# An attention and feed-forward block on one core: down weights fetched from ScalarE's queue, row subtractions kept out of three steps, rows taken in order

## The reference

```
x = x + layernorm(attn(layernorm(x)))        # 16 heads of 32, scores masked to one triangle
x = x + layernorm(ffn(layernorm(x)))         # silu(g) * u, 2048 wide, int32 weights with zero point 128

kqv = x @ Wqkv + bqkv;  scores = k q^T / sqrt(32), triangular mask;  out = softmax(scores) v;  out @ Wo + bo
g = x Wg^T;  u = x Wu^T;  h = silu(g) * u;  out = h Wd^T      # W = (int - 128) * scale of its row
```

## Time and profile before

| | |
|---|---|
| median of 3 runs | 1640.79 us (1640.74 to 1642.38) |
| the profiled execution: its time | 1639.89 us |
| its span | 1638.1 us |
| TensorE busy in the span | 94% |
| VectorE, ScalarE, GpSimd busy | 57%, 49%, 36% |
| the chain that ended last, by engine | TensorE 72%, VectorE 10%, GpSimd 6%, ScalarE 4%, SP's queue 3% |
| attention of the 16 groups | 87.6 to about 950 us |

### The profile page before, as it was taken

One profiled execution on the slowest core, in us unless ns is written; L12 is line 12 of the kernel. 1 busy time (PEld: TensorE's weight loads), 2 busy tenths in 40 slices (PEclk: granted clock), 3 DMA queues, 4 the chain that ended last, 5 costly groups with the idle time before them and its releaser, 6 DMA issues.

```text
span 1638.1 us, 24488 instructions
## 1 busy us (share of the span) xinstructions
PE 1544.6 (94%) x9322; PEld 641.2 (39%) x9324; DVE 939.4 (57%) x1864; ACT 795.9 (49%) x1284; POOL 592.7 (36%) x809
## 2 busy tenths in 40 slices
PE   4899999998999999999977999999999999999997
PEld 2333334333333333333322244444444444444443
DVE  5666755788756887667756333564434343434344
ACT  5356676667666776667755633232222222222222
POOL 4335664677556766755755310020000000000001
PEclk8999999999999999999988999999999999999999
DMA  4212322224411233223345431221111111111000
GB/s 181 92 50 52 77 55 53 67 64 117 105 48 35 81 106 88 61 52 95 106 137 164 108 97 45 59 97 38 47 26 52 26 52 26 52 26 52 1 26 26
DMA packets 113398, 112.26 MB, mean 69 GB/s; under 512 B 69632, under 2 KB 69632, under 8 KB 113024
## 3 DMA queue, kind: packets, MB, share of 16 engines
q1 hardware_dynamic: 113280, 110.69, 23.7%
HBM read 45.37 MB, written 25.17 MB: 43 GB/s over the span
## 4 chain that ended last, share of the span: by engine, by line
PE 72%; DVE 10%; POOL 6%; ACT 4%; issue 4%; SPq 3%; DMA 1%; POOLq 0%; ACTq 0%; DVEq 0%
PE ps L976 25%; PE ps L897 16%; PE ps L993 12%; PE ps L960 10%; PE ps L934 5%; DVE mcol L1255 4%; SPq L753 3%; POOL pt L1467 2%; PE ps L910 2%; ACT pt L1109 1%; POOL rs L1387 1%; PE ps L918 1%; DVE st L1150 1%; DVE xh L650 1%; POOL pt L1458 1%
## 5 line engine op out<-in xcount | busy, mean ns | idle before, releaser
L1109 ACT ACTIVATE pt<-ps,nrm 128x512 f32<-128x512 f32 (+1 forms) x640 | 361.5, 647 | 222.0 <-PE ps L934 208.8
L976 PE MATMUL ps<-x2in,gu 128*128 128x512 f16 x2048 | 462.4, 379 | 0.1
L1255 DVE TENSOR_REDUCE mcol<-ps 128x1 f32<-128x512 f32 (+2 forms) x636 | 318.0, 566 | 139.3 <-PE ps L918 93.1
L976 PEld LDWEIGHTS ps<-x2in,gu 128*128 128x128 f16 x2048 | 200.2, 98 | 242.0 <-ACT sg L1130 0.6
L1384 POOL TENSOR_SCALAR rs<-mv 128x1 f32<-128x1 f32 x120 | 27.2, 226 | 652.4 <-DVE mv L1154 646.1
L1326 DVE SCALAR_TENSOR_TENSOR hf<-ps,usc,sg 128x512 f32<-128x512 f32 x128 | 96.1, 751 | 259.1 <-PE ps L976 245.6
L1135 ACT ACTIVATE hh<-hf 128x512 f16<-128x512 f32 x128 | 80.7, 631 | 258.8 <-DVE hf L1326 245.2
L1467 POOL TENSOR_TENSOR pt<-pt 128x1024 f32<-128x1024 f32 x84 | 201.5, 2421 | 1.8 <-ACT pt L1109 1.8
L934 PE MATMUL ps<-qpack,kpack 98*128 98x512 f16 (+3 forms) x768 | 163.6, 331 | 29.0 <-DVE mcol L1255 25.7
L993 PE MATMUL ps<-wd,hh 128*128 128x512 f16 x496 | 188.0, 379 | 0.0
L993 PE MATMUL ps<-wd,hl 128*128 128x512 f16 x496 | 188.0, 379 | 0.0
(11 more groups left out here) (125 smaller groups left out, 1592.8 us busy)
## 6 DMA issues: line engine op xcount, KB each, us to landing
qpack<-stage SPq DMA_DIRECT2D x192, 64.0 KB, 2.0
kpack<-stage SPq DMA_DIRECT2D x192, 64.0 KB, 2.0
xr<-in_x SPq DMA_DIRECT2D x32, 256.0 KB, 2.9
x1d<-xr SPq DMA_DIRECT2D x32, 256.0 KB, 2.3
x2d<-xh SPq DMA_DIRECT2D x32, 256.0 KB, 2.3
x1in<-x1d SPq DMA_DIRECT2D x8, 1024.0 KB, 5.8
out_x<-yy SPq DMA_DIRECT2D x32, 256.0 KB, 2.0
xin<-in_x SPq DMA_DIRECT2D x24, 256.0 KB, 2.9
```

Of the source, the lines that this page charges most:

```text
L976: mm = pe.matmul(bk, GU[:, c, m, i * 128:(i + 1) * 128], x2in[:, 1 - k, p, c, :], start=p == 0 and c == 0, stop=p == 1 and c == 3)
L1109: act.activation(Pt[:, PBUF[step], h, off:512], ps[:, BANK[job], off:512], ACT.Exp, scale=esc).then_inc(s_ex, 1)
L1255: mm = dve.tensor_reduce(mcol[:, n % 2, col:col + 1], scores, AX.X, ALU.max)
```

## The change

Three things, all in the attention of the four batches.

1. The fetches of down-weight blocks 1 to 7 leave SP and go to ScalarE: `act_fetch i` stands at the start of the step behind the one in which block i-1 was converted, and first waits for that conversion.
2. In groups with g = 1 no turn is placed in steps 5, 6 and 7 (those in which GpSimd adds). And turns are taken only in the order in which their rows were normed; `untaken` is now a list.
3. In groups with g = 2 the projections are laid out otherwise: `qk` in steps 3, 5, 7, 9 instead of 1, 3, 7, 9, and the first `vproj` in step 1 instead of 0.

```diff
-        for i, s in enumerate(((0, 2, 3, 7) if b else (1, 3, 7, 9), (0, 1, 2, 3), (1, 3, 7, 9), (1, 2, 3, 8))[g]):
+        for i, s in enumerate(((0, 2, 3, 7) if b else (1, 3, 7, 9), (0, 1, 2, 3), (3, 5, 7, 9), (1, 2, 3, 8))[g]):
...
-        for i, s in enumerate(((), (7, 9), (0, 2, 4, 6, 8), (0,))[g]):
+        for i, s in enumerate(((), (7, 9), (1, 2, 4, 6, 8), (0,))[g]):
...
-    untaken = 0
+    untaken = []
...
-            if kind == "residual" and adding(step):
+            if adding(step) and (kind == "residual" or step // NS % 4 == 1 and kind in ("ln1_turn", "turn2")):
                 continue
...
-            if kind in ("ln1_norm", "norm2") and untaken == 2 or kind in cost and not free(kind, step) and (
-                    room.get(step, 99) < cost[kind]):
+            if kind in ("ln1_norm", "norm2") and len(untaken) == 2 or (
+                    kind in ("ln1_turn", "turn2") and untaken[0] != t):
                 continue
-            untaken += {"ln1_norm": 1, "norm2": 1, "ln1_turn": -1, "turn2": -1}.get(kind, 0)
+            if kind in cost and not free(kind, step) and room.get(step, 99) < cost[kind]:
+                continue
+            if kind in ("ln1_norm", "norm2"):
+                untaken.append(t)
+            if kind in ("ln1_turn", "turn2"):
+                untaken.pop(0)
...
             add(("step", n, s))
+            plan += [("act_fetch", i) for i in range(1, 8) if ffn_step(i - 1) + 1 == NS * n + s]
...
-                     for each in [("ffn_load", i)] + [("ffn_fetch", k) for k in range(24) if RAW_BEFORE[k] == i]]
+                     for each in [("ffn_load", i)] + [("ffn_fetch", k) for k in range(8, 24) if RAW_BEFORE[k] == i]]
...
+                elif kind == "act_fetch":
+                    i = a[0]
+                    e.wait_ge(s_cv["act"], i)
+                    ra, src, _ = raw_of_ffn(i)
+                    act.dma_start(ra, src).then_inc(d_raw[RAW[i]], 16)
```

## The result

The kernel after the change takes 1662.09 us in the median of its runs (1661.02 to 1662.61), beside 1640.76 for the kernel before on the same chip (1636.63 to 1642.38). The ratio is 1.0133, with a 95% interval of 1.0114 to 1.0152: slower by 21.3 us. The profiled execution took 1661.02 us with a span of 1659.3; before it was 1639.89 and 1638.1. The forecast was 1661.8 us.

A forecast was written before the change was run, and what follows sets the result against it. TensorE, with 72% of the chain that ended last, was taken as the bound. +29.2 - 0.5 - 5.7 - 2.0 = +21.0 on the profiled 1639.89 gave 1660.9, and 0.9 more for the median 1661.8 us; range 1651 to 1671.

The forecast's parts named there:

- What bounds: Whole kernel: TensorE carries 72% of the chain that ended last, so time is lost or won where TensorE waits.
- Part 1: Groups 6 and 10: ScalarE's copy for a turn waits some 14.5 us behind packs; +14.6 us each, +29.2 together.
- Part 2: Groups 2, 6 and 10: what the new layout wins and costs outside the stall, together -0.5 us.
- part 3: Groups 1, 5 and 9: no turns beside GpSimd's additions; -2.4 us each in 5 and 9, -0.9 in 1, sum -5.7.
- third case: turn2 5, now in (5,8), could meet GpSimd's last addition, some 2 us a subtraction; as a rival 1668 us, 10%.
- Part 4: Groups 12 and 13: packs(14) starts earlier, -3.7 us at (13,2); exposed fetches on ScalarE cost 0.6 each; sum -2.0.
- the turns don't stall: Rival for groups 6 and 10: ScalarE's copy isn't held, the 29.2 us goes; 1631 us, faster, 7%.
- the stall is partly refilled: Rival: VectorE, GpSimd and SP run ahead during the stall, no clock loss; 11.0 us each instead of 14.6; 1653 us, 12%.
- Contention at the new places: Rival: moved subtractions of groups 1, 5, 9 cost 2 us more each, half exposed, plus step 0's inversion; 1668 us, 10%.
- the fetches only cost: Rival: SP is held by something else at packs(14) and all seven issues are exposed, +3.7 + 2.5; 1668 us, 8%.

The follow-up runs named there:

- the fastest kernel: The kernel before with the change's row work and fetches, and packs 6, 7, 10, 11 and 14 moved late in the preceding group: 1618.95 us, ratio 0.986.
- the two missed attempts to cure it: Packs 6, 7, 10, 11, 14 moved to the end of step 4 of the preceding group: 1648.54 us on the changed kernel, 1644.15 on the kernel before.

## Why the prediction was right

**What bounds.** Right. No share of the page moved by more than 3 points, the stretch with the feed-forward layer took 690.9 us in both, and the loss lies in the two steps that the forecast named for it. Smaller differences in (6,7), (10,7), (1,8) and (9,2), and 0.7 in the start-up, it had not named.

**Part 1, the stall.** The mechanism was shown from three sides: the rules of the row work alone bring it, a third buffer moves it to another engine, and half of the issues halve it. Its size was right within a microsecond. ScalarE stood 14.96 and 14.78 us, 14.5 was forecast. Counted from the start of the exponentials of (5,9), packs(7) began after 4.33 us (forecast 4.66), and the exponentials of (6,1) after 24.74 (forecast 25.06). So the whole chain was right, with 0.3 us too much at its head. What was to be given back and what the clock was to cost lie in (6,1) and (10,1): the forecast put -1.6 and +2.6 there, so +1.0, and measured are +0.5 and +0.8. Which of the two terms was off can't be told apart. In the second window above TensorE was busy for 5.12 of 6.2 us at a clock of 0.58, so it was not the bound in all of it, which points to the clock as the term that was too high. In sum a stall was worth 13.8 us in group 6 and 13.9 in group 10, for 14.6.

**Part 2, the layout.** Right in size by luck, incomplete in its reasoning. The forecast for step 0 of group 2 was -0.75, and (2,0) grew by 1.04. The gain of a step 0 without its projection is real: with the new layout (10,0) takes 5.34 us in two kernels (three buffers; packs late in the group on the changed kernel), 0.63 less than the 5.97 of before. What the forecast lacked is the clock. TensorE waits the same 1.3 us in (2,0) of the changed kernel and in (10,0) of the second of these two, but only in the first does the granted clock then fall, at 205.3 us. The windows are (2,0) of the changed kernel, and (10,0) of the other with its waits:

```profile
202.23:209.25 7.02, 5.70 (x30) 1.61 (x29) 6.25 (x13) 3.15 (x6) 2.61 (x4) 0.76 0.40 98
```

```profile
642.17:647.51 5.34, 4.02 (x30) 1.42 (x29) 5.24 (x10) 4.36 (x7) 3.28 (x5) 1.00 0.67 153
```

```profile
PE ps L921 <- ACT pt L1120: 0.8, 1, 0.8
PE ps L971 <- POOL pt L1474: 0.5, 1, 0.5
```

Such a stretch at half clock lies in (2,0) in all seven kernels with the new layout, and in none of the six without it; in the kernel before TensorE is busy through the whole of it. Why (10,0) is sometimes spared is open. (2,2) gave 0.7 back and (2,5) took 0.95. Group 2 came to +1.0 for +0.5.

In groups 6 and 10, what lies outside the stall came to +0.5 and -0.4, where -0.75 and -0.25 were forecast. (10,3) lost 1.7 us, as forecast, but (6,3) only 0.8 of its 8.20, since a copy ahead of the next exponentials found its buffer's DMA not landed. And (6,7) took 1.4 us more (5.97 to 7.39), (10,7) as much, which the forecast had not: the `qk` of that step waits for tile 23, whose turn now stands in (6,6) and not in (6,4). The first row is ScalarE's at (6,3), the second TensorE's at (6,7):

```profile
456.50 0.63 ACT L1029 ACTIVATE xh<-xn 128x512 f16<-128x512 f32 x1 [1.22 <-DMA xT<-xh]
```

```profile
473.48 1.89 PE L903 MATMUL ps<-xT,wh 128*128 128x512 f16 x8 [1.27 <-DMA xT<-xh]
```

With the rules of the row work alone (6,3) is 5.65 and (6,7) 5.97, so both come only where the two parts are together. What makes tile 23 late is again the pair of part 3. Step (6,6) is one in which GpSimd adds, and the new rule keeps turns out of such steps only in groups with g = 1. The first two rows are the changed kernel's, addition and subtraction of tile 23; the third is the subtraction of the same tile in the fastest kernel, whose turn stands in the same step:

```profile
467.39 7.43 POOL L1478 TENSOR_TENSOR pt<-pt 128x1024 f32<-128x1024 f32 x3
```

```profile
467.46 2.83 DVE L656 TENSOR_TENSOR xh<-xn,xh 128x512 f16<-128x512 f32 x1
```

```profile
451.47 0.86 DVE L661 TENSOR_TENSOR xh<-xn,xh 128x512 f16<-128x512 f32 x1 [0.33 <-ACT xh L1034]
```

In the changed kernel the subtraction comes later in the step and lasts 2.0 us longer, and TensorE waits 1.27 of them. In all six kernels with both parts it takes 2.81 to 2.83 us, and in all three with the new rules and before's layout 0.85 to 0.87. That the copies of the `qk` in (6,5), new there, push ScalarE's copy back to beside the additions is my reading of the lists, not tested. The new layout paid in no kernel here: alone it cost 0.85 to 1.3 us a group.

**Part 3, no turns beside the additions.** The mechanism was right as far as it went and the size was close: (5,7) went from 9.88 to 7.17 and (9,7) from 9.88 to 7.16, 2.7 us each for 2.4 taken. GpSimd is the next limit, as forecast: TensorE now waits 1.14 us for it there. The neighbour that the term was taken from, (4,7) in the earlier trace rows, was the right one, but it held more than the forecast named. The kernel before has a stretch at half clock in (5,7), from 406.0 to 409.4 us, and another in (9,7), and neither (4,7) nor the changed kernel has one. The 12 projection matmuls of (5,7) took 4.45 us in it and take 2.76 now; the first eight of them before:

```profile
405.56 3.17 PE L897 MATMUL ps<-wh,xT 128*128 128x512 f16 x8
```

So up to 1.7 of the 2.7 us are clock that came back; it did so where the wait of 1.67 us ahead of the stretch had gone, but no run parts the two. In group 1 the forecast left this out: it gained 2.9 and not 0.9, and 2.0 of these lie in (1,8), in which the kernel before has such a stretch and the one after has none. Group 9 gained 1.0 in all, though (9,7) alone gave 2.7, since a stretch at half clock appeared in (9,2), which went from 7.12 to 8.42. These windows are, first, of before in group 1 and then, of after, in group 9:

```profile
192.00:200.00 8.00, 6.76 (x52) 2.71 (x52) 4.10 (x13) 4.90 (x10) 2.23 (x7) 0.79 0.50 116
```

```profile
613.00:620.00 7.00, 5.50 (x44) 2.67 (x45) 5.83 (x9) 5.06 (x9) 3.93 (x7) 0.76 0.61 151
```

A longer (9,2) with such a stretch stands in five more kernels with the same row work there and is missing in three others ((9,2) is 7.05 in the one with half of packs behind, 7.17 in the one with three buffers, 7.28 with the whole of packs behind). What decides it is open. The errors in groups 1 and 9 nearly cancel.

The Trainium skill's rule (SBUF — State Buffer, Who interferes with whom, the shared port pair) was carried into the forecast as a third case: turn2 5, in its new place, could meet the last addition. It does. The first row is GpSimd's, the second VectorE's, the third VectorE's next subtraction with nothing beside it:

```profile
406.18 2.38 POOL L1478 TENSOR_TENSOR pt<-pt 128x1024 f32<-128x1024 f32 x1
```

```profile
406.96 2.15 DVE L656 TENSOR_TENSOR xh<-xn,xh 128x512 f16<-128x512 f32 x1
...
413.44 0.68 DVE L656 TENSOR_TENSOR xh<-xn,xh 128x512 f16<-128x512 f32 x1
```

It took 1.5 us longer, and 1.6 us is what was left of the addition when it began (406.18 + 2.38 less 406.96), so the trace agrees with a wait for the end of one addition. The step (5,8) still lasted 5.59 us as before: VectorE had the slack. The contention is real, and here its price was nothing; in (6,6) and (10,6), which the third case did not name, it was not.

**Part 4, the fetches.** -1.5 us for -2.0. SP no longer waits for the conversions of down weights ahead of packs(14), as was forecast; one wait of 15.5 us for the last conversion is left, ahead of a fetch of a later block at 883.38. (13,2) came to 16.20 and not to 14.5, and with the fetches alone to 14.05. In the changed kernel packs(14) runs from 826.72; the first exponentials of group 13 come at 831.8, so it begins 5.1 us ahead of them where it had been 1.4 (807.42, and 808.8). But the load of tile 21, at 843.78, comes only 3.0 us earlier, for packs(14) itself took 17.1 us against 16.4:

```profile
826.72 6.18 SPq L759 DMA_DIRECT2D qpack<-stage  x8
...
843.78 0.53 SPq L722 DMA_DIRECT2D xr<-in_x  x1
```

Why the step then shrank by 2.0 and not by 3.0 is open. In kernels that leave everything up to (13,2) there as it was, the step took 16.64 and 17.54 us beside 18.21, so a microsecond of it is spread between executions. On ScalarE an exposed fetch cost 0.63 us, (12,3) going from 6.08 to 6.71, for 0.6 taken.

The other rule of the Trainium skill (DMA: Bandwidth & Descriptors, Issuing engines are not separate DMA queues) is that an issue from another engine saves only issue time, usually small. The runs decide as follows. (13,2) fell by 4.2 us with the fetches alone, seven times an issue, so the saving there is a queue that no longer waits. In (13,2) other profiles differ by 1.6 us without any such edit, so the 4.2 is uncertain by about that. Over both groups the rule's verdict of a small gain holds all the same: none that can be told from zero on the kernel before, 1.5 us in the changed kernel, some 2 in the fastest one.

**The rivals.** That the turns don't stall fell with the first timeline. That the stall is partly refilled fell too: groups 7 and 11 have their old lengths to 0.01 us, so nothing that ran ahead was kept. Contention at the new places was there: it cost nothing in (5,8), and the forecast missed the two places, (6,6) and (10,6), where TensorE waited 1.3 us in the next step for the tile; that the fetches only cost is refuted by (13,2). The errors of the terms are -2.0 in group 1, +0.5 in group 2, -0.5 in group 5, +1.4 in group 9, -1.5 for the two stalls, +1.1 for the rest of groups 6 and 10, +0.5 in groups 12 and 13, and +0.7 in the start-up. They add up to +0.2: 21.2 in the spans for 21.0. The sum is therefore better than its parts; with these errors, 2 or 3 us off would have been no surprise. Most of the misses outside the stall are of two kinds, stretches at half clock that came or went, and the subtraction of tile 23.

## What to carry to other kernels

In a list that several queues walk in order, a run of issues is an obstacle of fixed length: here 24 DMAs, 16 us. Before moving a job across it, or it across jobs, list what stands behind it in the new place and who waits for each of these; the loss of this change and the two missed attempts to cure it were the same oversight, made in three places. A change of several parts may be slower as a whole and still hold the faster kernel: taken apart and with the obstacle moved, two of its three parts gave 1.4% together with that move, of which the fetches' share is the least certain. And a projection with no one waiting for it may be the filler of a gap: moved out, it made step 0 shorter by 0.6 us where the clock stayed up, and 0.4 to 1.1 longer where the opened gap was followed by a stretch at half clock. When steps are compared, look at the granted clock in both before giving the difference to a job.

## What the runs showed of the hardware

- A run of 24 DMA issues on SP in one piece took 15.1 to 17.3 us in the attention, so 0.63 to 0.72 each. The same eight issues take 4.96 us at one time and 6.2 at another, in kernels with and without fetches on ScalarE; what makes them slower is open.
- A DMA that ScalarE issues takes 0.37 to 0.44 us to issue and 0.51 us of idle time in front of the next instruction; with the overlap that is lost, 0.63 us of a gapless stretch.
- Stretches at half clock, 3.4 us long, come and go, among others at 194.4, 406.0, 627.9 and 863.4 us in the kernel before and at 205.3, 423.7, 614.9 and 884.5 in the one after. Some go with a layout: (1,8) and (5,7) have one in the kernels with the old row work and in none with the new, (2,0) in all with the new projections and in none with the old. In (9,2) and (1,8) such a stretch went with 1.3 and 2.0 us. Around the stalls behind packs they are 3.4 to 13.7 us long.
- A subtraction on VectorE of 0.68 us takes 2.8 beside GpSimd's additions, 467.46 and 467.39 above.
- The start-up, the same code in every kernel here, took 84.8 to 90.4 us in the profiled executions. That is more than most of the terms of the sum, and the reason to compare lengths of groups and not spans alone.
